# Long convolution of a first stage in two blocks of 128 tokens instead of one of 256

## The reference, cut to what matters

```python
def s4d(x, log_dt, A_re, A_im, C_re, C_im, D_skip):
    ...
    K = 2.0 * jnp.einsum('dn,dnl->dl', dC, powers).real
    n = 2 * L
    Kf = jnp.fft.rfft(K, n=n, axis=-1)
    xf = jnp.fft.rfft(x, n=n, axis=1)
    y = jnp.fft.irfft(xf * Kf.T[None], n=n, axis=1)[:, :L]
    return y + x * D_skip
...
scores = jnp.where(vision_mask[:, None, None, :], scores, -jnp.inf)
topv, topi = jax.lax.top_k(scores, K_TOP)
probs = jax.nn.softmax(topv, axis=-1)
...
x = layernorm(x_text, g_norm_in, b_norm_in)
x = x * (1.0 + mod_gate * scale_in) + mod_gate * shift_in
y = s4d(x, log_dt, A_re, A_im, C_re, C_im, D_skip)
y = y * (1.0 + mod_gate * scale_out) + mod_gate * shift_out
xt = x_text + y
h = layernorm(xt, g_ffn, b_ffn)
h = jax.nn.gelu(h @ W1 + b1, approximate=False) @ W2 + b2
```

## Time and profile before

| | us |
|---|---|
| median of 3 runs | 1381.75 (1381.48 to 1383.94) |
| span of the profiled execution | 1503.4 |
| that execution's own time | not given; its span is 121.7 above the median of the runs |
| PE busy | 1203.0 (80%) |
| DVE busy | 887.9 (59%) |
| ACT busy | 580.3 (39%) |
| POOL busy | 466.2 (31%) |

### The profile page before, as it was taken

One profiled execution on the slowest core, in us unless ns is written; L12 is line 12 of the kernel. 1 busy time (PEld: TensorE's weight loads), 2 busy tenths in 40 slices (PEclk: granted clock), 3 DMA queues, 4 the chain that ended last, 5 costly groups with the idle time before them and its releaser, 6 DMA issues. The chain is left out here.

```text
span 1503.4 us, 24492 instructions
## 1 busy us (share of the span) xinstructions
PE 1203.0 (80%) x7028; PEld 869.8 (58%) x7032; DVE 887.9 (59%) x2553; ACT 580.3 (39%) x1116; POOL 466.2 (31%) x749
## 2 busy tenths in 40 slices
PE   2597999999857756584958793868999989999997
PEld 1395677777646545373746672655666645555554
DVE  8998999999234643452625363565766634453534
ACT  2324566665322113252635331634666641212110
POOL 2237344555450336326141704622221000000000
PEclk9858999999979978697978896876999999999999
DMA  9000000000007412383823731625100000000000
GB/s 267 0 2 1 1 1 1 1 1 1 1 8 192 143 43 80 107 252 97 262 80 91 259 101 56 96 70 136 16 13 10 2 1 1 14 0 14 0 14 15
DMA packets 92463, 91.98 MB, mean 61 GB/s; under 512 B 27057, under 2 KB 77747, under 8 KB 92341
## 3 DMA queue, kind: packets, MB, share of 16 engines
q1 hardware_dynamic: 80052, 65.32, 14.5%
q0 software_dynamic: 12288, 25.18, 6.8%
HBM read 75.79 MB, written 14.68 MB: 60 GB/s over the span
## 5 line engine op out<-in xcount | busy, mean ns | idle before, releaser
L2263 PE MATMUL gq_psH<-gq_xT,gq_w 128*128 (+1 forms) x564 | 102.9, 309 | 53.3 <-ACT gq_act L1981 28.4
L2263 PEld LDWEIGHTS gq_psH<-gq_xT,gq_w 128*128 128x128 f32 x564 | 83.4, 209 | 81.6 <-issue 76.6
L3503 ACT ACTIVATE m_silu<-m_psG 128x512 f32<-128x512 f32 x48 | 28.7, 597 | 215.3 <-PE m_psU L3623 215.3
L2273 PE MATMUL gq_psY<-leaf_w,gq_hT 128*128 (+1 forms) x282 | 95.2, 422 | 20.0 <-issue 14.3
L3556 DVE TENSOR_TENSOR m_act<-m_silu,m_psU 128x512 f32<-128x512 f32 x48 | 33.0, 687 | 122.5 <-ACT m_silu L3503 107.7
L1865 POOL DMA_INDIRECT gq_x<-rows_x,gq_token_i x48 | 47.0, 979 | 174.0 <-PE gq_psX L2252 105.6
L3623 PE MATMUL m_psG<-m_xnT,m_gate 128*128 128x512 f32 x192 | 91.2, 597 | 2.1 <-PEq L192 2.1
L3623 PE MATMUL m_psU<-m_xnT,m_up 128*128 128x512 f32 x192 | 91.4, 599 | 0.0
L2149 DVE SCALAR_TENSOR_TENSOR gq_hT<-gq_xT,unit_leaf,gq_act 128x128 f32<-128x128 f32 x141 | 49.6, 352 | 61.7 <-issue 28.6
L1981 ACT ACTIVATE gq_act<-gq_psH,leaf_b 128x128 f32<-128x128 f32 x141 | 51.4, 365 | 75.4 <-remote 41.5
L783 DVE MATCH_REPLACE8 s_product_a_rest<-a_top,s_product_a_rest 128x256 f32<-128x256 f32 x192 | 76.1, 408 | 0.3 <-issue 0.3
(11 more groups left out here) (574 smaller groups left out, 3063.6 us busy)
## 6 DMA issues: line engine op xcount, KB each, us to landing
leaf_w<-in_group_w SPq DMA_DIRECT2D x128, 128.0 KB
leaf_w<-in_group_w SPq DMA_DIRECT2D x64, 256.0 KB
a_w<-in_L_xattn_W SPq DMA_DIRECT2D x2, 1024.0 KB, 11.9
rows_x<-token_rows SPq DMA_DIRECT2D x8, 256.0 KB, 5.4
sorted_y_q<-gq_y SPq DMA_DIRECT2D x16, 128.0 KB, 3.9
sorted_y_k<-rows_ahead SPq DMA_DIRECT2D x16, 128.0 KB, 4.4
sorted_y_v<-gq_y SPq DMA_DIRECT2D x16, 128.0 KB, 1.7
rows_f<-token_rows SPq DMA_DIRECT2D x8, 256.0 KB
```

The costliest lines, as they stand in the source:

```text
L2263: last = pe.matmul(psH[n % 2][:, 0:P], w1[n % 3][:, c, :], xT[:, c, bass.ds(g * -P + u * P, P)], start=(c == 0), stop=(c == DC - 1))
L2273: pe.matmul(psY[n % 3][:, 0:D], hT[n % 2][:], weights.w2[:, bass.ds(g * D, D)], start=True, stop=True).then_inc(y_ps, 1)
```

## The change

The 256 tokens of a sequence are taken as two blocks of 128. Both blocks are transformed at once with length 256 (128 frequencies): two matmuls of 128x512 in place of eight of 128x256. The first block of the result is block 0 times the kernel's own spectrum; the second is block 1 times the same spectrum plus block 0 times the spectrum of the kernel advanced by 128 tokens. The latter is made once, in step 0, from the kernel's second 128 values and its first spectrum with alternating signs (`shifted_spectrum`, four POOL instructions of 128x256). POOL's products become six instructions of 128x512 and eight of 128x256, with a signal after the sixth (`y_first`) and one at the end; the one-column copy goes. PE's inverse transform is two matmuls that wait for `y_first` and two that wait for the end. The tables are the even rows of the old ones: the forward one and the kernel's are loaded so (the latter by 16 DMAs into a buffer that POOL blanks first), the inverse one is thinned out by a POOL copy before step -1. DVE makes the signs with two one-column instructions in the setup. PE's forward transform and ACT's copy of the spectrum now stand ahead of the whole up projection and of all gelus.

```diff
-        load(dft[:], self.dram["dft"], self.late)
-        load(idft[:], self.dram["idft"], self.late)
+        even = self.dram["dft"].rearrange("(p two) t k f -> two t p k f", two=2)
+        for t in range(ST):
+            load(dft[t * P // ST:(t + 1) * P // ST], even[0, t, :, :, 0:P], self.late)
+        load(idft_in[:], self.dram["idft"][:, 0], self.late)
...
+                def shifted_spectrum():
+                    pool.wait_ge(signs, 3)
+                    pool.wait_ge(spectrum_in, 2)
+                    across = shift[:, 0:1].to_broadcast([P, D])
+                    do.mark(pool.tensor_tensor(turn[:, 0], ki[:, 0], across, ALU.mult))
+                    do(pool.tensor_tensor(turn[:, 1], kr[:, 0], across, ALU.mult))
+                    do.mark(pool.tensor_tensor(kr[:, 1], kr[:, 1], turn[:, 0], ALU.subtract))
+                    do(pool.tensor_tensor(ki[:, 1], ki[:, 1], turn[:, 1], ALU.add))
+                def block_products(m):
...
+                    for n, (a, k) in enumerate(four):
+                        do.mark(pool.tensor_tensor(part[n], x[a], own[k], ALU.mult))
+                    released(pool, y_ps, m)
+                    do.wait()
+                    do(pool.tensor_tensor(y[0], part[0], part[1], ALU.subtract))
+                    pool.tensor_tensor(y[1], part[2], part[3], ALU.add).then_inc(y_first.s, 1)
+                    reached(pool, y_first, m)
+                    for n, (a, k) in enumerate(four):
+                        do.mark(pool.tensor_tensor(part[n][:, 0], x[a][:, 0], shifted[k], ALU.mult))
+                    do.wait()
+                    do.mark(pool.tensor_tensor(part[0][:, 0], part[0][:, 0], part[1][:, 0],
+                                               ALU.subtract))
+                    do(pool.tensor_tensor(part[2][:, 0], part[2][:, 0], part[3][:, 0], ALU.add))
+                    do(pool.tensor_tensor(y[0][:, 1], y[0][:, 1], part[0][:, 0], ALU.add))
+                    pool.tensor_tensor(y[1][:, 1], y[1][:, 1], part[2][:, 0], ALU.add
+                                       ).then_inc(y_sb.s, 1)
...
+                        if m == 0:
+                            shifted_spectrum()
                         reached(pool, spec_sb, m)
...
+                        block_products(m)
...
+                pool.wait_ge(late, 16 * N_LATE)
+                pool.tensor_copy(idft[:], idft_in[:, :, 0:S:2]).then_inc(idft_set, 1)
                 step(-1)
...
+                dve.tensor_scalar(shift_i[:], shift_i[:], 1, None, ALU.bitwise_and
+                                  ).then_inc(signs, 1)
+                dve.wait_ge(signs, 2)
+                dve.tensor_scalar(shift[:], shift_i[:], -2.0, 1.0, ALU.mult, ALU.add
+                                  ).then_inc(signs, 1)
...
                         for t in range(ST):
+                            reached(pe, (y_first, y_sb)[t], m)
                             for part in range(2):
-                                for k in range(2):
...
+                                last = pe.matmul(pA[:, t, :], idft[:, part],
+                                                 yspec[:, part, t * D:(t + 1) * D],
+                                                 start=(part == 0), stop=(part == 1))
```

More of the change, by code:

```diff
@@ L302, in first_stage @@
         sq = [sb(f"s4_square{n}", [P, 2, HD]) for n in range(2)]
+        turn = sb("s4_turned_spectrum", [P, 2, D])
         ksb = sb("s4_K", [P, D, NCP // 4])
@@ L401, in _ @@
                 weights.load(sp)
-                sp.dma_start(kdft[:], dram["kernel_dft"]).then_inc(kdft_in, 16)
+                even = dram["kernel_dft"].rearrange("(q c a n) d k f -> q c n a d k f", q=2, c=2,
+                                                    n=2)[:, :, :, :, 0, :, 0:P]
+                sp.wait_ge(kdft_blank, 1)
+                for q in range(4):
+                    for half in range(2):
+                        at = NA * q + NA // 2 * half
+                        for c in range(2):
+                            sp.dma_start(
+                                kdft[at:at + NA // 2, c, :, half * P:(half + 1) * P],
+                                even[q % 2, c, q // 2]).then_inc(kdft_in, 16)
             @block.gpsimd
@@ L471, in add_skip @@
                     pool.tensor_tensor(k0, k0, dskip[:], ALU.add).then_inc(kevac, 1)
+                def shifted_spectrum():
[7 more added lines that the diff above has]
+                def block_products(m):
+                    x, y, part = ([t[:, n].rearrange("p (j d) -> p j d", j=2) for n in range(k)]
+                                  for t, k in ((spec, 2), (yspec, 2), (prod, 4)))
+                    own = [t[:, 0:1].to_broadcast([P, 2, D]) for t in (kr, ki)]
+                    shifted = [t[:, 1] for t in (kr, ki)]
+                    four = ((0, 0), (1, 1), (0, 1), (1, 0))
+                    released(pool, y_sb, m)
+                    for n, (a, k) in enumerate(four):
[14 more added lines that the diff above has]
+                                       ).then_inc(y_sb.s, 1)
                 def step(i):
@@ L687, in step @@
                                 "p a s -> p (a s)"), ACT.Copy).then_inc(fout_sb.s, 1)
-                    if has(e):
-                        gelus(e, range(HC // 2))
                     if has(m):
@@ L695, in step @@
                     if has(e):
-                        gelus(e, range(HC // 2, HC))
+                        gelus(e, range(HC))
                     if has(f):
@@ L739, in _ @@
                 for t, ps in ((kr, pC), (ki, pH)):
[L740 removed]
+                    act.activation(t[:], ps[:], ACT.Copy, scale=2.0).then_inc(spectrum_in, 1)
                 for t in range(ST):
@@ L1231, in step @@
                             film_tile(1, t, flat((pB, pC)[t][:])).then_inc(fout_ps.s, 1)
-                    if has(e):
-                        reached(pe, hT_sb, e)
-                        up(e, range(HC // 2))
                     if has(m):
@@ L1237, in step @@
                         for part in range(2):
-                            for k in range(2):
-                                for t in range(ST):
-                                    last = pe.matmul(pW[:, part, k, :],
-                                                     dft[:, t, part, k * P:(k + 1) * P],
-                                                     x1[:, t, :], start=(t == 0),
-                                                     stop=(t == ST - 1))
+                            last = pe.matmul(flat(pW[:, part]), dft[:, part],
+                                             x1[:].rearrange("p t d -> p (t d)"), start=True,
+                                             stop=True)
                         last.then_inc(spec_ps.s, 1)
                     if has(e):
-                        up(e, range(HC // 2, HC))
+                        reached(pe, hT_sb, e)
+                        up(e, range(HC))
                     if has(f):
@@ L1275, in step @@
                         for t in range(ST):
+                            reached(pe, (y_first, y_sb)[t], m)
                             for part in range(2):
-                                for k in range(2):
-                                    last = pe.matmul(pA[:, t, :],
-                                                     idft[:, k, part, t * P:(t + 1) * P],
-                                                     yspec[:, part, k * D:(k + 1) * D],
-                                                     start=(part == 0 and k == 0),
-                                                     stop=(part == 1 and k == 1))
+                                last = pe.matmul(pA[:, t, :], idft[:, part],
+                                                 yspec[:, part, t * D:(t + 1) * D],
+                                                 start=(part == 0), stop=(part == 1))
                         last.then_inc(y_ps.s, 1)
```

39 lines of the change are left out of this document (17 added, 22 removed).

## The result

The change makes the kernel slower by 0.7%: 1390.51 us (median of 20 runs, 1383.12 to 1405.74) against 1381.43 us (20 runs), ratio **1.0071 [1.0053, 1.0089]**. The forecast was 1392 us, 1381 to 1402, and slower with a chance of 0.74. Two single runs, 1622.98 us of the kernel before and 1405.74 of the one after, were slow executions and are left out of the ratio. The profiled execution took 1397.19 us (span 1395.1, so 2.1 us around it), 6.7 above the median: its marks show more than the typical loss. So the first stage of the earlier trace rows is sound.

A forecast was written before the change was run, and what follows sets the result against it. DVE's top-32 search sets the pace with PE close behind; in the drain PE is the bound. Terms 5.6 + 3 + 1 + 0.5 = +10 us on the median of 1381.75 gave 1392 us, range 1381 to 1402.

The forecast's parts named there:

- step 0: POOL's longer queue delays the inverse transform's second half, so DVE gets the film later: +5.6 us, bounds +1.8 and +13.
- clock: Steps 2 to 6: PE idling before attention turns loses clock, 0.6 us a step, +3 us; bounds 0 and +10.
- step 4: POOL's second part of the products meets DVE's pair products and L808: +1 us, bounds 0 and 1.5.
- drain: After the last search, PE's shorter transforms gain 3 us but low clock costs 3 to 4: +0.5, bounds -3 and +3.
- behind the first stage: Everything after the first stage: the change touches nothing there, so no term in the sum.
- the mutual hold-up: Step 0: POOL's eight 256-column instructions and DVE's two-input products delay each other 0 to 3.7 us; half taken.
- PE's saving: Shorter transforms take 3.5 us off each step on PE; buys nothing in steps 1 to 6, time in the drain.
- gelu wait: PE's new wait in the up projection, whose fifth chunk needs ACT's first two gelus: 0.7 us.
- Idle before the turns: PE idles 3.5 us instead of 0.68 before each attention turn in steps 2 to 6, about 6.0 before the drain's.
- Rival 2: Faster, 1375 us: clock falls inside steps before the change too, so PE bounds and 2.8 us per step counts; chance 0.12.

The follow-up runs named there:

- tables early: Kernel after the change with 13 of POOL's table-building instructions moved into an earlier wait; 1381.81 us, 1.0011 of the kernel before.
- blanking late: Kernel after the change with POOL's blanking of the transform buffer put behind its other setup memsets; one run, no ratio measured.
- inverse repeated: Kernel after the change with PE computing the inverse transform twice in steps 1 to 5, three times in step 6; 1.0030 of the kernel before.
- three cures: Kernel after with tables early, blanking late, inverse repeated fitted to each step: 0.9928 of before, again 0.9970; with 12 more matmuls behind the last inverse 0.9966.

## Why the prediction was right, step by step

It named the mechanisms and the sign; that the sum of +10 met +9.1 is partly luck, because its errors offset. The two profiles of the kernel after give, in that order:

| term | predicted | against before's first profile | against its second |
|---|---|---|---|
| step 0 | +5.6 (1.8 to 13) | +8.6, +8.6 | +8.6, +8.6 |
| steps 1 to 6: clock, step 4 | +3, +1 (0 to 11.5) | +7.8, +5.4 | +6.2, +3.7 |
| drain | +0.5 (-3 to +3) | +3.0, -0.7 | -2.4, -6.2 |
| behind the first stage | 0 | not comparable | -4.6, -2.7 |

So the sign of the drain's term depends on which profile of the kernel before it is held against.

- **Step 0, mis-sized.** POOL's second signal was predicted at 158.0 and came at 161.65. 2.2 of the 3.7 us arose before the products, which began at 145.01 and not 142.85: 0.9 from the blanking at the start (shown by moving it), the rest from two-column instructions under DVE's products. Three of them were slowed by 3.0 us in all (the two shown, and one of 0.24 that took 1.19), where before one was, by 0.8; POOL's tables behind them took 0.8 less. 1.5 arose in the products, where I took half of the mutual hold-up; the rows of L515 show it whole. (The Trainium skill, SBUF — State Buffer, Who interferes with whom, says that a DVE instruction with two SBUF inputs contends with a GpSimd instruction that reads SBUF, and that the contention is an exclusive lock; by it the prediction had 159.8. The trace agrees: 1.59 us for an instruction of 0.72.) That the first mark follows POOL's queue is shown by the tables moved ahead, -7.6 us.
- **PE's saving is off the path in the steps.** Forward 1.88, inverse 1.89 for eight, gelu wait 0.70: as predicted. Idle before the turns was 2.9 to 3.1 us in steps 2, 3, 4 and 6 and 1.3 in step 5, predicted 3.5. That idle time costs the clock was right; its size was not: +3, where steps 1 to 6 without step 4 lost 6.5 and 3.8 us against the first profile of before. With PE filled these steps have the old length, which shows that the clock is the loss there.
- **Step 4.** POOL's second part met DVE's pair products as predicted, and the price of 1 us was about right: DVE was busy 1.2 us longer, and the step was 1.3 and 1.6 us longer. PE's wait of 1.9 us for that part was not in the sum, and DVE did not wait for it; PE then idled another 1.31 us for DVE, and its turn ran at the low clock. Step 4 before and, below, after:

```profile
267.38:304.99 37.61, 35.55 (x178) 26.98 (x178) 35.73 (x128) 22.96 (x44) 21.41 (x36) 1.00 0.00 1
```

```profile
278.53:317.41 38.88, 34.22 (x158) 24.50 (x158) 36.97 (x127) 22.87 (x44) 27.79 (x43) 0.95 0.01 1
```

- **Drain.** Idle 4.84 (predicted 6.0), then turn, context and film slow, as predicted. With the clock held it is 2.4 us shorter than before (predicted 3); without, 3.0 longer or 0.7 shorter than in before's first profile.
- **A hidden assumption failed and did no harm.** I took the gelu wait as free for DVE. It is nearly free only because the shorter forward transform pays for it: alone, the reorder costs 0.5 to 1.1 us in each of steps 1 to 5, 5 us in the whole time.
- **Rival 2 was half right.** In its second profile the kernel before also ran at the low clock, in the turns of step 1 and of the drain. If its timed executions do so as well, of which no trace was kept, the difference is smaller than the +19 and +13 us between the last marks. It did not inside steps 2 to 6 (five turns of 2.02 us in either profile), so the shorter transforms bought nothing there.

The part behind the first stage stays open: with whole-length transforms it took 961.7 to 966.9 us in four profiles, with half-length ones 959.6 to 963.9 in nine. Nothing there is changed, and no run was made to tell why; so its -4.6 and -2.7 us have no known cause.

## What to carry to other kernels

Work taken off an engine that is second in line turns into idle time; on TensorE that idle time can cost the clock of the work behind it, so price it, and see whether something may fill it. Filling gave 6.0 us where PE had 3 us of idle time in a step, and nothing where it had 0.7. A split adds small instructions to another engine's queue: look where that queue is already late (here the first step) and which of its neighbours' instructions will meet the new ones. Two profiles of one kernel differed by 7 us at a mark where nothing was changed: read two before a term of a few us is called measured.

## What the runs showed of the hardware

- The same idle time had both outcomes: behind 3.33 and 3.34 us at the drain's turn, and behind 2.86 us twice at the turn of step 2, PE kept the high clock once and lost it once. Behind 3.76 us the turn of step 4 ran at the high clock in "tables early" and at the low one in "blanking late":

```profile
269.85 2.02 PE L1249 MATMUL a_psW<-identity,s_Z_re_a_pair 128*128 128x128 f32 x16 [3.76 <-DVE s_Z_re_a_pair L856]
```

```profile
276.30 3.75 PE L1245 MATMUL a_psW<-identity,s_Z_re_a_pair 128*128 128x128 f32 x16 [3.76 <-DVE s_Z_re_a_pair L852]
```

The idle time alone does not decide it. In these two and the two profiles of the kernel after, 13 of the 20 turns of steps 2 to 6 took more than the 2.02 us of the high clock, that of step 5 and that of the drain in all four; in the four profiles with PE filled (inverse repeated and the three with three cures) 2 of 20 did.
- The time of an execution goes with its granted clock. For 75 executions of the kernel before, the span rises by 0.34 us for each us at the low clock (worked out as 2 x (1 - clock) x span), with a correlation of 0.90. Its mean clock was 0.930, or 192 us low; that of 19 executions of the kernel after, without that of 1405.74 us, 0.917, or 230 us. 38 us more, by 0.29 (the slope of the kernel after) to 0.34, are 11 to 13 us, an estimate: somewhat more than the whole difference. It is a correlation: PE idles longer in step 0 of the kernel after, at a clock of 0.50 to 0.52, so part of the low time comes from the lateness and does not cause it.
- A memset of 128x2048 on POOL held DVE's first instruction until its own end: the same instruction took 2.32 us after, 1.44 with the blanking late and 1.30 before, and 0.23 later on without a memset beside it.
- 128x256 f32 on POOL with two tensor inputs took 0.72 us, with one and a column for the other 0.61, a strided copy 0.40; 128x512 1.26.
